# First expert's rows summed with the residual and written plainly; bias split and two sums of squares moved to GpSimd; keys copied ahead of roots

## The reference

```python
qp, kp, vp = norm(x) @ Wq.T + bq, ctx @ Wk.T + bk, ctx @ Wv.T + bv
kh, vh = l2_normalize(kp by head), l2_normalize(vp by head)
x = x + q @ (kh.T @ vh)
```

## Time and profile before

| what | us |
|---|---|
| median of 3 runs (lowest, highest) | 392.17 (390.69, 395.66) |
| the profiled execution | 392.03 |
| its span | 390.2 |
| busy PE, PEld | 305.2 (78%), 259.3 (66%) |
| busy DVE, ACT, POOL | 227.4 (58%), 217.6 (56%), 215.1 (55%) |
| mean granted clock of PE | 0.88 of full |

### The profile page before, as it was taken

How to read it: one execution, slowest core, us unless ns; L and a number is a source line. 1 busy time by engine, 2 the same in 40 slices (tenths; PEclk the granted TensorE clock), 3 DMA queues, 4 the chain that set the end, 5 groups by cost and what they waited for, 6 DMA issues and landing times. The chain is left out here.

```text
span 390.2 us, 6948 instructions
## 1 busy us (share of the span) xinstructions
PE 305.2 (78%) x2323; PEld 259.3 (66%) x2323; DVE 227.4 (58%) x899; ACT 217.6 (56%) x432; POOL 215.1 (55%) x191
## 2 busy tenths in 40 slices
PE   5888778786696596777986999969898798969800
PEld 4556556664375366456675899969888797969700
DVE  4788877979476765784788555544545263524300
ACT  1978837657284454563443666745756476736500
POOL 3000564166557446365700486868686877858682
PEclk9999969799696696696599999998999899989965
DMA  5703233061341613012015445546474647454342
GB/s 193 278 3 108 68 88 137 9 215 53 95 167 55 197 40 123 30 35 87 16 70 165 110 35 109 83 68 127 47 149 35 157 41 159 35 104 34 29 34 20
DMA packets 23939, 35.21 MB, mean 90 GB/s; under 512 B 4173, under 2 KB 16074, under 8 KB 23904
## 3 DMA queue, kind: packets, MB, share of 16 engines
q0 software_dynamic: 14400, 11.16, 20.0%
q1 hardware_dynamic: 8928, 23.27, 17.8%
q10 hardware_dynamic: 576, 0.33, 0.3%
HBM read 18.82 MB, written 16.66 MB: 91 GB/s over the span
## 5 line engine op out<-in xcount | busy, mean ns | idle before, releaser
L452 POOL DMA_INDIRECT out_dram<-y_sb,token x80 | 123.7, 1547 | 64.3 <-issue 32.8
L413 POOL DMA_INDIRECT slots_dram<-rows,place_no x90 | 87.8, 976 | 103.0 <-DVE place_no L788 47.4
L889 DVE SCALAR_TENSOR_TENSOR hid_lo<-ps,hid_hi 128x1024 fp32r<-128x1024 f32 x39 | 47.8, 1225 | 65.6 <-ACT hid_hi L571 59.9
L1038 PE MATMUL ps<-xgt_hi,wi_hi 128*128 128x256 f32 x160 | 52.8, 330 | 0.8 <-DVE xgt_lo L850 0.8
L949 PE MATMUL ps<-wkv_sb,ct_sb 128*128 128x256 f32 x128 | 42.3, 432 | 9.9 <-ACT kvb L509 6.9
L1047 PE MATMUL ps<-hid_hi,wo_hi 128*128 128x256 f32 x160 | 48.4, 303 | 1.3 <-DVE hid_lo L889 0.7
L1039 PE MATMUL ps<-xgt_lo,wi_hi 128*128 128x256 f32 x160 | 46.3, 289 | 0.0
L1040 PE MATMUL ps<-xgt_hi,wi_lo 128*128 128x256 f32 x160 | 46.2, 289 | 0.0
L1049 PE MATMUL ps<-hid_hi,wo_lo 128*128 128x256 f32 x160 | 45.6, 285 | 0.0
L1048 PE MATMUL ps<-hid_lo,wo_hi 128*128 128x256 f32 x160 | 45.5, 285 | 0.0
L571 ACT ACTIVATE hid_hi<-ps 128x1024 fp32r<-128x1024 f32 x39 | 40.0, 1025 | 4.7 <-PE ps L1040 2.3
(11 more groups left out here) (126 smaller groups left out, 640.0 us busy)
## 6 DMA issues: line engine op xcount, KB each, us to landing
xg<-slots_dram SPq DMA_DIRECT2D x8, 576.0 KB, 4.0
out_dram<-rows SPq DMA_DIRECT2D x7, 576.0 KB, 3.2
x_sb<-x_dram SPq DMA_DIRECT2D x7, 512.0 KB, 5.8
ct_sb<-ctx_t_dram SPq DMA_DIRECT2D x7, 512.0 KB, 8.4
wi_sb<-w_in_dram SPq DMA_DIRECT2D x8, 256.0 KB
wo_sb<-w_out_dram SPq DMA_DIRECT2D x8, 256.0 KB
slots_dram<-rows,place_no POOLq DMA_INDIRECT x90
out_dram<-y_sb,token POOLq DMA_INDIRECT x80
```

The lines of the kernel that those rows point to most:

```text
L413: pool.indirect_dma_start(slots[:, :], bass.IndirectOffsetOnAxis(ap=place_no[:, u % PLACES_RING, j:j + 1], axis=0), rows[:, c % ROWS_RING, ...
L452: pool.indirect_dma_start(out_parts, bass.IndirectOffsetOnAxis(ap=token[:, e, j:j + 1], axis=0), y_sb[:, e % 2, j, :], None, compute_op=AL ...
L889: dve.scalar_tensor_tensor(hid_lo[:, i % 2, :], [ps0, ps1][i % 2][:, :], 0.0, hid_hi[:, i % 2, :].bitcast(F32), ALU.max, ALU.subtract).the ...
L1038: pe.matmul(bank, w_hi, xgt_hi[:, i % 2, :], start=True, stop=False)
```

## The change

- Expert 0: DVE, not ACT, makes `y_sb`, as the turned result times the gate plus the row's own x1, which still lies in `xg` (`first_outputs`, a new function in DVE's loop). POOL writes these rows without the addition.
- The bias split goes from DVE to POOL. A part is cast straight to its own row (0, 32, 64) of a zeroed `bkv_rows`, in place of a masked product over all partitions.
- For steps 2 and 3 (`POOL_SUMS`) POOL makes the sums of squares, as three additions that halve the eight numbers of a head, and the guard.
- In every step without a logit part ACT copies keys and values ahead of the roots. In step 0 it copies `xnt` ahead of the squares, and makes the next `xn` ahead of `qt`.
- PE runs 52 idle products at the start instead of 24, and for chunk 0 all four projections, then the turning of `xn`, then the four bias products.

```diff
+POOL_SUMS = (2, 3)
...
+            def split_biases():
+
+                pool.wait_ge(bias_loaded, 16)
+                left = bkv_sb[:, :]
+                for r in range(3):
+                    row = slice(32 * r, 32 * r + 1)
+                    order.add(pool.tensor_copy(bkv_rows[row, :], left[row, :]))
+                    order.wait()
+                    if r < 2:
+                        order.add(pool.tensor_copy(bkv_part[:, r, :], left))
+                        order.wait()
+                        order.add(pool.tensor_tensor(bkv_rest[:, r, :], left, bkv_part[:, r, :], ALU.subtract))
+                        order.wait()
+                        left = bkv_rest[:, r, :]
+                pool.sem_inc(bias_ready, 1)
+
+            def sum_squares(s):
+
+                squares = sq[:, :, :, :].rearrange("p g a (h i) -> p (g a h) i", i=HD)
+                sums_of = ss[:, :, :, :].rearrange("p g a h -> p (g a h)")
+                after(pool, kv_squared, s)
+                order.add(pool.tensor_tensor(fours[:, :, :], squares[:, :, 0:4], squares[:, :, 4:8], ALU.add))
+                order.wait()
+                order.add(pool.tensor_tensor(twos[:, :, :], fours[:, :, 0:2], fours[:, :, 2:4], ALU.add))
+                order.wait()
+                after(pool, kv_rooted, s - 1)
+                order.add(pool.tensor_tensor(sums_of, twos[:, :, 0], twos[:, :, 1], ALU.add))
+                order.wait()
+                pool.tensor_scalar(sums_of, sums_of, L2_EPS * L2_EPS, None, ALU.max).then_inc(norms_ready, 1)
...
+            split_biases()
+            for s in POOL_SUMS:
+                sum_squares(s)
...
+                    if e == 0:
+
+                        pool.indirect_dma_start(
+                            out_parts, bass.IndirectOffsetOnAxis(ap=token[:, e, j:j + 1], axis=0),
+                            y_sb[:, e % 2, j, :], None,
+                        ).then_inc(rows_added[e % 2], 16)
...
                 if valid(s):
+                    after(act, state_summed, s - 2)
+                    act.copy(kvb[:, s % 2], ps_kv).then_inc(kv_copied, 1)
                     if u is None:
                         roots(s)
-                    after(act, state_summed, s - 2)
-                    act.copy(kvb[:, s % 2], ps_kv).then_inc(kv_copied, 1)
...
-                if 0 <= y:
+                if GROUPS <= y:
                     e = y // GROUPS
...
-                if valid(s):
+                if valid(s) and s not in POOL_SUMS:
                     sum_squares(s)
...
+            def first_outputs(y):
+
+                after(dve, gates_made, 0)
+                after(dve, y_turned, y)
+                for q in range(PAIR):
+                    j = y * PAIR + q
+                    ins = dve.scalar_tensor_tensor(y_sb[:, 0, j, :],
+                                                   ps3[:, 512 * (y % 2) + PG + P * q:512 * (y % 2) + PG + P * (q + 1)],
+                                                   gate[:, 0, j:j + 1], xg[:, 0, j, 0:D], ALU.mult, ALU.add)
+                ins.then_inc(y_made, 1)
+
+            for i in range(1, ALL_GROUPS + 2):
+                t, y = i + 1, output_at(i)
+                if 0 <= y < GROUPS:
+                    first_outputs(y)
...
-            idle_products(24)
+            idle_products(52)
```

More of the change, by code:

```diff
@@ L451, in _ @@
                         after(pool, y_made, e * GROUPS + j // PAIR)
[L452 to L455, removed]
+                    if e == 0:
[3 more added lines that the diff above has]
+                        ).then_inc(rows_added[e % 2], 16)
+                    else:
+                        pool.indirect_dma_start(
+                            out_parts, bass.IndirectOffsetOnAxis(ap=token[:, e, j:j + 1], axis=0),
+                            y_sb[:, e % 2, j, :], None, compute_op=ALU.add,
+                        ).then_inc(rows_added[e % 2], 16)
             pool.drain()
@@ L497, in _ @@
                     act.wait_ge(small_loaded, 16 * 4)
+                if s == 0:
+                    after(act, x_turned, s)
+                    act.copy(xnt[:, :], ps_t).then_inc(xnt_made, 1)
                 if valid(s):
@@ L807, in step @@
                     choices_of(late)
[L809 to L826, removed]
             def low_part(e, which):
@@ L880, in _ @@
             low_part(1, 1)
[L881 to L882 removed]
+            def first_outputs(y):
[11 more added lines that the diff above has]
+                    first_outputs(y)
+                if i >= ALL_GROUPS:
+                    continue
                 if t < ALL_GROUPS:
@@ L909, in centre_wi, with turn_input @@
                 pe.matmul(centred(e), centre[:, :], wi_sb[:, e % 2, :], start=True, stop=True).then_inc(wi_centred, 1)
+            def turn_input(n):
+                after(pe, x_normed, n)
+                for g in range(G):
+                    ins = pe.transpose(ps_t[:, P * g:P * (g + 1)], xn[:, n % 2, g, :], ident[:, :])
+                ins.then_inc(x_turned, 1)
             for s in STEPS:
@@ L1000, in _ @@
                     idle_products(16)
-                if valid(n):
-                    after(pe, x_normed, n)
+                if valid(n) and n > 0:
                     if valid(l):
                         after(pe, x1t_made, l)
-                    elif valid(s):
+                    else:
                         after(pe, xnt_made, s)
-                    for g in range(G):
-                        ins = pe.transpose(ps_t[:, P * g:P * (g + 1)], xn[:, n % 2, g, :], ident[:, :])
-                    ins.then_inc(x_turned, 1)
+                    turn_input(n)
             idle_products(5)
```

33 lines of the change are left out of this document (23 added, 10 removed).

## The result

The changed kernel took 379.8 us (median of four runs, 378.5 to 381.4) against 392.95 us for the kernel before (four runs). The ratio is 0.968, with a 95% interval from 0.964 to 0.972. In a later group, next to other kernels on one chip, it took 384.3 us against 393.8: ratio 0.976, interval 0.969 to 0.982. The forecast was 382, in a range from 376.5 to 389.

The account below looks back on a forecast made before the run. POOL's scatters were taken to bound the last 149.5 us, with attention steps ahead in which no engine is full. Savings of 1.5 + 1.7 + 4.0 + 2.6 = 9.8 us from 392.0 gave 382 us, range 376.5 to 389.

Parts of the forecast that it names:

- start: First norm and projections: bias split off DVE lets squares of chunk 1 start at 15.7 instead of 17.2, saving 1.5 us.
- steps 2 and 3: Early attention steps: keys copied ahead of the root and sums on POOL save 1.7 us, between 0 and 2.6.
- keys ahead of roots, later: Steps 5, 7, 9, 11, 13: PE no longer waits for ACT's copy, saving 4.0 us, between 0 and 5.5.
- expert 0: Expert 0's scatters: without the addition, expert 1 starts 2.6 us earlier, the middle of 1.9 and 3.2.
- the rival with the low clock: Start: projections stay at 1.19 us, so the start loses 1.0 us instead of giving 1.5; 384.5 us, chance 8%.
- the cover: Step 2: 3.9 us between squares of chunk 2 and ACT wanting the norms, 0.9 more than POOL's sums take.
- the residual waits in more than four places: Attention steps: a sign of being wrong, DVE's residual waits in more than four places or above 20.4 us in sum.
- the rival with shrinking waits: Attention steps: the four waits of 5.1 us shrink by themselves, 5 us gone, 377 us; chance 8%.
- the middle case of the forecast: Expert 0's last scatter: saving of 2.6 us, between landing as before (1.9) and a sooner landing (3.2).
- Plain scatters at 1.54 us: Expert 0: scatters without addition still cost 1.54 us, because the destination's rows of 16 are dear; 384.6 us, chance 5%.
- POOL's sums late: Steps 2 and 3: sums take 6 us each instead of 3.0, norms come 2 us late; 386 us, chance 4%.
- Bursts that set the pace: Attention steps: scatter bursts set the pace, so the 4.0 us don't arrive; 386 us, chance 17%.

Follow-up runs that it names:

- the second profile: The changed kernel run again unaltered, as reference of the second group, against the kernel before: 384.3 us, ratio 0.976.
- the eight early ones: Changed kernel with the sums of steps 2 and 3 on DVE and eight extra POOL additions of 512 numbers a partition; 348.6 us, 0.975 of the kernel before.

## Why the prediction held, term by term

| term | forecast | measured | where |
|---|---|---|---|
| start | 1.5 | 2.03 | squares of chunk 1 |
| steps 2 and 3 | 1.7 | 1.97 | squares of chunk 4 |
| keys ahead of roots, later | 4.0 | 4.67; 2.0 in the second profile; 1.4 by the means of nine profiles | first scatter |
| expert 0 | 2.6 | 2.24; 2.27 | first scatters, experts 0 and 1 |
| behind it | 0 | -0.31 | |
| sum | 9.8 | 10.6; 8.5 | span |

The sum came out near, but its largest term is not shown at its size, so that part is luck as far as the record goes. The start, steps 2 and 3, expert 0 and the stretch behind it are read from rows that repeat from profile to profile.

- **What bounds the end.** That the last 149.5 us follow rigidly from expert 1's first scatter held in all thirteen profiles that have the additions, on both chips: 148.8 to 150.8 us. Some have one expert boundary that is a microsecond longer. POOL is the bound, but at most 2 us per expert ahead of the next one, which the profile before did not tell.
- **The start** gave 0.5 us more than forecast. Squares of chunk 1 were to stand at 15.7 and stood at 15.15: `xn` was done at 8.97 for 9.1 and the bias products at 10.1 for 10.5, and everything behind them is 0.3 to 0.5 us early. The added idle products are worth 1.0 us, where the rival with the low clock had taken 2.5: PE lost 1.53 us rather than 2.0 on the projections, and these weren't the last thing in the chain. The other 1.0 us is shared by the bias split and the new orders of step 0, which were not undone one at a time.
- **Steps 2 and 3** came out near, by a wrong split. I gave 1.0 us to the copy's order and 0.7 to the sums on POOL. Undone one at a time, the order costs about 1.5 us here and the sums 0.19. POOL's price of 3.0 us a step was right (3.05 and 3.08), and the cover held, by 0.4 us at step 2 (done at 24.58, asked for at 24.99) and 2.9 at step 3. Two things failed. ACT's wait for PE's turning, which swallowed the first sum's gain, was not in the forecast. And the additions were to cost nothing elsewhere: the changed kernel shows their price on DVE, 0.83 us for an instruction of 0.18. The Trainium skill (GPSIMD Engine Reference, section 2) has one SBUF read port shared by GpSimd and DVE. The longer DVE instruction is in line with that, though no run separates the port from other causes. I had it as a rival against POOL's own time, where no effect is seen (1.27 us for the first addition in both steps). It was DVE that paid. By 2.6 cycles an element, from section 3.1 of the same page of the Trainium skill, 896 results would take POOL an estimated 1.9 us and dispatch. The three additions took 2.28 us.
- **Keys ahead of roots, later.** PE's waits for the copy went, as forecast, and came back when only the order was undone, with about 4 us of time, 1.9 of it by the squares of chunk 4. What is left behind them is 2.1 us by the medians and 1.4 by the means of the profiles, and noise allows anything between nothing and the 4.0. That 4.0 was three quarters of 5.5 us by judgement, and in this stretch one profile of the same kernel differs from another by as much as the term. The sign "the residual waits in more than four places" did come (seven), and the unnamed waits as a whole went from 10 to 16 places. At the same time the residual's waits of over 5 us fell from four to two, as the rival with shrinking waits had it. So the waits both spread and shrank, and their sum does not follow the time: with the sums on DVE the residual's are 12.9 us and with 24 idle products 9.6, and attention is no shorter there (first scatters at 212.3 and 211.2).
- **Expert 0** came within 0.4 us. Pair 4 is scattered 16.06 us behind the first scatter (forecast 16.0); then one more scatter's step of 1.26, 0.96 for itself and 2.06 for the landing make 20.34. The landing is 0.4 us shorter than with additions, the middle case of the forecast. DVE's new waits delayed nothing that shows.
- **The rivals.** Plain scatters at 1.54 us and POOL's sums late are refuted by rows above. So is a low clock at the start, by projections of 1.97 us; the granted clock reads 1.00 there whatever they take, so it decides nothing. Bursts that set the pace, so that the later 4.0 us don't arrive, is not refuted: on the first chip the late signals are tied to bursts, and the order's worth behind chunk 4 is not clear of noise.

## What to carry to other kernels

When an engine that ends the kernel gets cheaper at its work, ask how far behind it the next one stands: here 5.7 us saved on POOL were worth 2.2 us, and about the same saving on each of the other experts 1.2 on average. A computation moved to GpSimd has two prices, its own time and what it adds to DVE's instructions beside it; look for the latter by comparing single DVE durations. A stretch in which many short waits hand over to each other varies by as much as a small change is worth, so read a change from the places where the trace repeats to 0.1 us, and where there is none, take several profiles of each kernel before giving the term a size.

## What the hardware showed that I had not expected

- The same kernel took 394 us on one chip and 358 us on another. With the changed order and sums, the traces agree to 0.1 us up to 36 us (squares of chunk 4 at 36.63 and, without pacing, 36.65) and then part: `qt` of chunk 8 is made at 89.6 and 91.4 us in the changed kernel's two profiles, and at 82.5 without pacing on the other chip. The difference goes with waits of up to 7.7 us that the profile can't name, 36 to 67 us in sum on the one chip and none on the other; the granted clocks are close (0.90 and 0.92 as means). What causes them stays open. That on the slower chip they go together with POOL's bursts is shown for one kind of place; why the other chip has bursts without them is not.
- An addition of 512 numbers a partition on POOL takes 1.27 us (1.16 in the eight early ones), of 256 0.61, of 128 0.40; a maximum over 128 takes 0.52 to 0.56, a cast of 256 to bf16 0.40, and on a single partition 0.39, no less.
- A DVE instruction of 0.18 to 0.23 us took 0.63 to 0.83 us beside such an addition; most others beside it, with more to do, took no longer than without.
